# A selective-scan layer with soft-routed experts: a separate buffer for VectorE's product with C, pair-sized dt buffers, the softplus chains placed part by part, y gated in its gate's buffer

## The reference

```
xf, res = split(x @ in_proj.T)                  # 512 channels each
xf = silu(conv(xf));  xb = silu(conv_b(xf))     # causal, 4 taps
per direction (xb: reversed in time):
  delta, B, C = split(u @ x_proj.T)             # 16 states
  dt = softplus(delta @ dt_proj.T + bias)
  dA = dt * A;  dA_cum[l] = exp(sum of dA after l)
  xs = cumsum(dt * u * B * dA_cum) / (dA_cum + 1e-12)
  y  = sum over the states of xs * C,  + u * D
y = (y + y_b) * silu(res);  x1 = layernorm(x + y @ out_proj.T)
x1n = layernorm(x1) * g + b;  logits = x1n @ slots_n.T    # 1024 slots
dispatch = softmax over rows;  combine = softmax over slots
per expert (16, of 64 slots): gelu(s @ Wg + bg) * (s @ Wu + bu) @ Wd + bd
out = layernorm(x1 + combine @ experts)
```

## Time and profile before

| | us |
|---|---|
| median of three runs | 6382.84 (6379.36 to 6392.4) |
| profiled execution | 6391.75 |
| its span | 6389.9 |
| POOL, DVE busy | 4857.2, 4887.0 |
| first scan of the loop, last scan | 99.7, 5290.0 |

### The profile page before, as it was taken

How to read it: one execution, slowest core, us unless ns; L and a number is a source line. 1 busy time by engine, 2 the same in 40 slices (tenths; PEclk the granted TensorE clock), 3 DMA queues, 4 the chain that set the end, 5 groups by cost and what they waited for, 6 DMA issues and landing times. The chain is left out here.

```text
span 6389.9 us, 71120 instructions
## 1 busy us (share of the span) xinstructions
PE 5305.4 (83%) x14640; PEld 2615.8 (41%) x14640; DVE 4887.0 (76%) x4310; ACT 4299.3 (67%) x6698; POOL 4857.2 (76%) x2327
## 2 busy tenths in 40 slices
PE   6878788888878787888888878787878787999977
PEld 2333333333333333334343434343434344555566
DVE  6988888888888888888888888888888882222233
ACT  4878787878778777878787878787878784111100
POOL 3999999999999999999999999999999991000000
PEclk9999998988989888889898989898989898999988
DMA  2434333333333333434343433333333332322266
GB/s 78 123 118 122 120 120 114 120 120 118 120 115 121 115 122 115 122 111 124 114 122 111 124 117 121 115 117 117 121 118 120 121 123 82 95 84 86 75 217 210
DMA packets 555713, 755.58 MB, mean 118 GB/s; under 512 B 124059, under 2 KB 272411, under 8 KB 553245
## 3 DMA queue, kind: packets, MB, share of 16 engines
q1 hardware_dynamic: 555293, 752.04, 38.0%
HBM read 662.04 MB, written 89.82 MB: 118 GB/s over the span
## 5 line engine op out<-in xcount | busy, mean ns | idle before, releaser
L637 POOL TENSOR_TENSOR g_ring<-dtu,b_ring 128x1024 f32<-128x1024 f32 x1026 | 2523.2, 2462 | 148.2 <-DVE e_ps L1008 107.2
L1008 DVE TENSOR_TENSOR_SCAN e_ps<-e_ps,g_ring 128x1024 f32<-128x1024 f32 x1024 | 2342.9, 2288 | 109.0 <-ACT e_ps L802 72.7
L646 POOL TENSOR_TENSOR v_ring<-z_ring,c_ring 128x1024 f32<-128x1024 f32 x896 | 2191.0, 2446 | 144.8 <-PE y_ps L1175 109.4
L1175 PE MATMUL y_ps<-v_ring,ident 128*128 128x512 f32 x3596 | 2036.0, 677 | 305.1 <-POOL v_ring L646 293.4
L802 ACT ACTIVATE e_ps<-dt,a_neg 128x512 f32<-128x512 f32 x2050 | 1398.6, 682 | 808.1 <-DVE z_ring L1025 635.2
L812 ACT ACTIVATE f_ring<-rsum,consts,a_neg_half 128x512 f32<-128x512 f32 x2050 | 1645.6, 803 | 0.8
L1025 DVE SCALAR_TENSOR_TENSOR z_ring<-f_ring,e_ps 128x1024 f32<-128x1024 f32 x896 | 1089.6, 1216 | 388.6 <-PE y_ps L1175 267.9
L1175 PEld LDWEIGHTS y_ps<-v_ring,ident 128*128 128x128 f32 x3596 | 704.8, 213 | 1186.2 <-issue 754.2
L1110 PE MATMUL side<-u,conv_diag 128*128 128x512 f32 x1088 | 503.7, 607 | 31.6 <-ACT rowT_ring L733 31.6
L1285 ACT ACTIVATE x_act<-x_gate,x_bg 128x512 f32<-128x512 f32 x128 | 87.9, 687 | 562.2 <-PE x_gate L1317 562.2
L1140 PE MATMUL side<-seT,xnT 128*128 128x512 f32 x544 | 308.9, 704 | 122.9 <-ACT xnT L727 102.4
(11 more groups left out here) (137 smaller groups left out, 5688.5 us busy)
## 6 DMA issues: line engine op xcount, KB each, us to landing
b_ring<-bc_scr SPq DMA_DIRECT2D x1027, 256.0 KB, 3.4
c_ring<-bc_scr SPq DMA_DIRECT2D x1025, 256.0 KB, 3.3
pT_scr<-rowT_ring SPq DMA_DIRECT2D x136, 256.0 KB, 3.5
m_pT<-pT_scr SPq DMA_DIRECT2D x16, 2048.0 KB, 8.4
sT_scr<-sT_ring SPq DMA_DIRECT2D x272, 64.0 KB, 2.5
x_xT<-sT_scr SPq DMA_DIRECT2D x16, 1024.0 KB, 8.8
eo_scr<-x_eo SPq DMA_DIRECT2D x32, 512.0 KB, 5.1
m_eo<-eo_scr SPq DMA_DIRECT2D x16, 1024.0 KB, 11.0
```

Of the source, the lines that this page charges most:

```text
L637: pool.tensor_tensor(g_ring[:, k], dtu[d][:, pair:pair + 2], both(b_ring[:, k:k + 1]), ALU.mult).then_inc(g_done, 1)
L646: pool.tensor_tensor(v_ring[:, k], z_ring[:, k], both(c_ring[:, k:k + 1]), ALU.mult).then_inc(v_pool, 1)
L1008: dve.tensor_tensor_scan(e, e, g, 0.0, ALU.mult, ALU.add).then_inc(scan_done, 1)
L1175: pe.matmul(y_ps[:, t % 2], ident[:], v, start=(t % (TILES // PAIRS) < 2), stop=True, skip_group_check=True).then_inc(v_used, 1)
```

## The change

Five things are changed, all in `sequence_stage`:

- DVE's product with C goes to a buffer of its own, `v_own`, and PE reads it there. DVE's product waits for PE's use of its previous product. The wait of z for a `z_ring` buffer is now always for POOL.
- `dt`, `dtu` and `rsum` hold one pair of chunks for each direction. Chunk i is at i % 2.
- The table of slots has another order, and `slot_tiles` spreads the slots between given tiles (`EARLIEST`). The dt pairs begin at tiles 1, 34, 66 and 97 (before: 2, 18, 43, 97).
- `yg` is `res_gate`: y is gated in place. res_0 and res_1 leave the slots made ahead (tiles 114, 116); all four res slots come after the out slots, at tiles 13, 16, 20, 23 (res_2 and res_3 before: 12, 15). `X_STEP` is 17.
- The slot embeddings are normalized in `g_ring` instead of `dt[0]`. PE's dt1_0 also waits for the bank of the slot before it.

Some more tiles, before and after: in0_0 31, 37; conv0_0 and conv0_1 37, 39 and 43, 44; rowsT_0 and rowsT_1 41, 42 and 46, 47; colsT_0 47, 48; conv1_0 and conv1_1 52, 54 and 52, 53; x0 88, 89; conv1_2 and conv1_3 91, 93 in both; the last slot 122 in both.

```diff
     order = """
-        dt1_0 dt1_1 out0 out1 res2 res3 dt0_2 dt0_3 xnT0 xnT1
-        rows0 rows1 in0_0 in0_1 cols0 cols1 conv0_0 conv0_1 rowsT0 rowsT1 dt1_2 dt1_3 colsT0 colsT1 rows2 rows3
-        conv1_0 conv1_1 slots0 slots1 cols2 cols3 rowsT2 rowsT3 colsT2 colsT3 rows4 rows5 slots2 slots3 cols4 cols5
-        in0_2 in0_3 rowsT4 rowsT5 conv0_2 conv0_3 colsT4 colsT5 x0_0 rows6 conv1_2 conv1_3 rows7 dt0_0 dt0_1
-        slots4 slots5 x1_0 cols6 cols7 rowsT6 rowsT7 res0 res1 colsT6 colsT7 slots6 slots7"""
+        dt1_0 dt1_1 out0 out1 res0 res1 res2 res3 xnT0 xnT1
+        rows0 rows1 dt0_2 dt0_3 in0_0 in0_1 cols0 cols1 conv0_0 conv0_1 rowsT0 rowsT1 colsT0 colsT1 rows2 rows3
+        conv1_0 conv1_1 slots0 slots1 cols2 cols3 rowsT2 rowsT3 colsT2 colsT3 rows4 rows5 dt1_2 dt1_3 slots2 slots3
+        cols4 cols5 in0_2 in0_3 rowsT4 rowsT5 conv0_2 conv0_3 colsT4 colsT5 x0_0 rows6 conv1_2 conv1_3 rows7 dt0_0 dt0_1
+        slots4 slots5 x1_0 cols6 cols7 rowsT6 rowsT7 colsT6 colsT7 slots6 slots7"""
...
+EARLIEST = {("dt1", 0): 1, ("out", 0): 8, ("xnT", 0): APPLY_TILE + 2, ("dt0", 2): 34, ("dt1", 2): 66, ("in0", 2): 79,
+            ("dt0", 0): 97, ("slots", 7): 122}
+
+
+def slot_tiles(table):
+
+    anchors = [s for s, slot in enumerate(table) if slot in EARLIEST]
+    tiles = []
+    for s, slot in enumerate(table):
+        first = max(a for a in anchors if a <= s)
+        after = min([a for a in anchors if a > s], default=first)
+        tile = EARLIEST[table[first]]
+        if after > first:
+            hold = [HOLD[kind] for kind, _ in table[first:after]]
+            tile += int((EARLIEST[table[after]] - tile) * sum(hold[:s - first]) / sum(hold))
+        tiles.append(max([tile] + tiles[-1:] + [t + 2 for t in tiles[-2:-1]]))
     return tiles
...
-    SP_LAG, X_STEP = 4, 10
+    SP_LAG, X_STEP = 4, 17
...
-        dt = [sb(f"dt{d}", [P, KI, L]) for d in range(NDIR)]
-        dtu = [sb(f"dtu{d}", [P, KI, L]) for d in range(NDIR)]
-        rsum = [sb(f"rsum{d}", [P, KI, L]) for d in range(NDIR)]
+        dt = [sb(f"dt{d}", [P, 2, L]) for d in range(NDIR)]
+        dtu = [sb(f"dtu{d}", [P, 2, L]) for d in range(NDIR)]
+        rsum = [sb(f"rsum{d}", [P, 2, L]) for d in range(NDIR)]
         sp_exp, sp_one = dtu, rsum
-        yg = sb("yg", [P, KI, L])
+        yg = res_gate
...
-                    dve.wait_ge(side_free[at.bank(s)], at.freed(s, 1 - SLOTS // 2))
+                    dve.wait_ge(side_free[at.bank(s)], at.freed(s, 1 if p == 0 else 1 - SLOTS // 2))
...
                 def z_slot_free(i):
 
-                    user = before(i)
-                    if on_dve(user):
-                        dve.wait_ge(v_used, b * TILES + (2 * (user + 1) + CR))
-                    else:
-                        dve.wait_ge(v_pool, b * (STEPS - len(ON_DVE)) + (pool_steps(user + 1) + CR))
+                    dve.wait_ge(v_pool, b * (STEPS - len(ON_DVE)) + (pool_steps(last_on_pool(before(i)) + 1) + CR))
...
-                    z_slot_free(i)
-                    dve.tensor_tensor(z_ring[:, k], e_ps[:, i % 2], both(c_ring[:, k:k + 1]), ALU.mult).then_inc(v_dve, 1)
+                    dve.wait_ge(v_used, b * TILES + (2 * (dve_step_before(i) + 1) + CR))
+                    dve.tensor_tensor(v_own[:], e_ps[:, i % 2], both(c_ring[:, k:k + 1]), ALU.mult).then_inc(v_dve, 1)
...
+                    if (kind, i) == ("dt1", 0):
+                        pe.wait_ge(side_free[at.bank(s - 1)], at.freed(s - 1))
...
-                v = (z_ring if on_dve(i) else v_ring)[:, RING[i % STEPS], t % 2]
+                v = v_own[:, t % 2] if on_dve(i) else v_ring[:, RING[i % STEPS], t % 2]
```

58 lines of the change are left out of this document (22 added, 36 removed).

## The result

The changed kernel takes 6341.46 us (median of five runs, 6329.01 to 6359.75), beside 6391.55 for the kernel before in the same comparison: ratio 0.9927, 95% interval 0.9909 to 0.9944. That is 47 to 50 us won. The forecast was 6297 and a gain of 86 to 95: the direction was right and the time lies in the range, but about half of the expected gain is missing. The question of the experiments is where it went.

The account below looks back on a forecast made before the run. POOL was taken as the bound, busy 303 of about 326 us a sequence, so five waits priced the change: 5.4 us times 16 = 86, from 6391.75 to 6306, then 6297 for the median; range 6165 to 6450.

Parts of the forecast that it names:

- PE 7.7 to 7.2: POOL's idle time from PE's use of v buffers: expected to fall from 7.7 to 7.2 us a sequence.
- the feedback: DVE's own wait on PE had been feeding back into PE's next bank; PE's 7.7 us was left at 7.2.
- the denser turns: PE's turns 43 to 57: 37.1 us of work in the new order, against 35.4 us that POOL needs.
- POOL's load is now the larger in each part: After moving chains, POOL's part loads 83.0, 75.0, 75.0, 70.1 us against DVE's 73.1, 74.9, 72.2, 66.5.
- As the number of such instructions is unchanged, the rule puts nothing into the sum: Two-SBUF-input DVE instructions and GpSimd ones exclude each other; their number is unchanged, so this adds nothing to the forecast.
- The premise that I had set to be tested: Stretching of POOL's instructions is constant: POOL's busy time in the kernel stays within 0.5% of 4857 us.
- The parts: A sequence's four parts of 16 steps: first near 88 us, third near 79, second 78 to 83.
- The reading of the clock: Second part 77.4 or 83.8 us: a few us of half-speed matmuls cost POOL 6.7 us of idle time.
- Rival 3: Slower: PE becomes the bound in turns 43 to 57 and again 83 to 95; 6447 us, chance 0.20.
- Rival 2: The wait only changes hands, POOL waiting for the same late PE one step later; 6383 us, chance 0.12.
- Rival 1: Evening out works fully, DVE never holds POOL, 10 us of 23 idle remain; 6175 us, chance 0.15.
- the stretching: Lengthening of POOL's instructions beside softplus chains; an estimated 1.9 us moves from the first part to the third.

Follow-up runs that it names:

- res_own: res_only with DVE's product with C in a buffer of its own and nothing else; 6253.73 us.
- res_only: The kernel before with all four gate slots together after the out slots and y gated in place, old chains and buffers; 6367.73 us.
- dt1late: res_own with the second pair of dt1 alone moved from tile 43 to 64, part two to part three; 30 us more than res_own.
- res_own_yield: res_own with POOL waiting, before its next product, until DVE's softplus fix step is done; 6228.27 us, ratio 0.9752.
- dt0late: res_own with the second pair of dt0 alone moved from tile 20 to 31, part one to part two; 114 us more than res_own.
- bothlate: res_own with the second pairs of dt0 and dt1 both moved later, old slot function and four-chunk buffers kept; 151 us more than res_own.

## Why the prediction was right or wrong

**What bounds the kernel: right.** In every run POOL is busy for 92 to 96% of a sequence, and its busy time stays within 297 to 303 us. Its idle time after, by the releasers in the groups by line divided by the number of sequences (products g over 64: 9.2, 9.3 and 9.5), beside what was forecast:

```
wait, us a sequence      before   forecast   after   res_own
v on z                    2.2       0          0       1.0
g on the scan             7.3       4.0        9.5     4.9
v on PE                   7.7       7.2        3.4     0.7
B row                     2.5       2.5        2.5     2.0
dtu on rsum               2.7       3.3        4.1     2.6
no releaser shown         0.1       0.1        1.4     1.7
```

**The product's own buffer: right in kind, too small.** z's wait on PE and POOL's wait on z went, as said. But the buffer was worth 114 us on top of the gate's part, not the 86 that all parts were to give. The term that undersized it is "PE 7.7 to 7.2": the feedback, that DVE standing still frees PE's next bank late and PE then holds POOL, is named there, but the denser turns were set against it and half a microsecond was left. From res_only to res_own v's wait on PE falls from 3.3 to 0.7 us a sequence. The larger fall, from 7.7 to 3.3, had come with the gate's slots before that, for which nothing was taken. The scan's wait fell by 2.1 with the buffer alone (7.0 to 4.9), where 3.3 was forecast.

**The softplus chains moved: the step that failed.** I had put the moved chain at POOL's load (two dtu and 1.9 us of stretching, 4.3 us in all), since "POOL's load is now the larger in each part", and had the scan's wait fall. It rose to 9.5 us. The parts one and two together went from 174.9 to 164.6 (-10.3), the parts three and four from 151.0 to 158.1 (+7.1), and dt1late shows the same with one chain alone, -9.2 and +11.8. The long fix isn't all of it: with POOL's wait in both kernels the third part still is 11.0 us longer with the chain than without (78.4 and 67.4). So the moved chain costs its part about DVE's 9.4 us and not POOL's 4.3. The reason fits the rows, but wasn't isolated: the scans that POOL waits for stand behind the chain in DVE's queue, even where DVE isn't full: in the changed kernel's third part it is busy 72.90 of 79.40 us, near the 72.2 forecast. The load of an engine over 16 steps didn't say what a burst of it costs within three.

**"As the number of such instructions is unchanged, the rule puts nothing into the sum": wrong.** Their number is unchanged, their cost is not. It depends on how many products POOL has ready at that moment. The fix took 8.2 us a sequence before and 16.8 after, up to 10.42 at step 20, and taking the shut-out away wins 77 us in the changed kernel and 51 in the one before. So part of the gain seems to be given back by what brought it: once POOL waits less, it runs its products without gaps, and a fix that needs a gap finds none (12.9 to 18.1 us from res_only to res_own). That this is worth the 26 us between 77 and 51 isn't clear of noise. The premise that I had set to be tested, POOL's busy time within 0.5%, moved by -0.6% only. It was the wrong engine to look at; the stretch is in DVE's row L932.

**The parts.** The first, the third and the second were forecast at 88, 79 and 78 to 83; measured on the mean are 81.7, 79.4 and 82.9. The second and third are as said. The first is 6 us better: in the window shown POOL is busy 77.4 us of it, where 83.0 was forecast, since the window holds 46 instructions of POOL instead of 50. For the fourth the prediction gives POOL's load alone, 70.1; the forecast sequence of 320.5 us leaves 70.5 to 75.5 for it, and it took 78.7. Its fix at step 52 takes 4.91 us on average, where it took 1.43. But this isn't all: with the fix at 1.75 in res_own_yield the part still takes 79.0. Part of the difference is POOL's lead at the cut, which this view can't separate.

**The reading of the clock.** The prediction laid all of the 6.7 us between two second parts (77.4 and 83.8) to half-speed matmuls. The fix took 1.21 us in the first of them and 3.38 in the second, so some 2 us can be its own. After, the same two parts are 80.7 and 85.3 long, and the fix took 5.76 and 10.40, which is as large a difference, at the same clocks as before (0.96 and 0.92). What the clock costs POOL by itself isn't shown by these pairs.

**The gate's slots and y in place:** I had taken nothing; res_only has 0.9976 (0.9964 to 0.9988), 15 us faster. POOL's wait on PE fell from 70.4 to 30.4 us in 3000, of which 12.2 came back as idle time before g with no releaser (1.0 to 13.2). xT's later load cost nothing that shows.

**The rivals.** Rival 3, PE as the bound in turns 43 to 57, did not come about: v's wait on PE fell, and half of the conv's matmuls less wins 1.2 to 2.5 us a sequence. In dt0late and bothlate, with a chain beside the conv fills, its mechanism does appear (66.8 and 61.8 us). Rival 2 fell with it. Rival 1, "DVE never holds POOL", is what res_own comes close to without any evening out: 13.6 us of idle time left a sequence, against the 10 that were worked out for it; and 12.5 with the yield. Of the 13.6, 5.9 still are waits on the scan and z.

**The sum.** Idle time fell by 1.3 us a sequence and POOL's busy time by 1.8, the sequence by 3.2, times 16 = 51, beside 47 to 50 measured. That this comes so close is luck: the two profiled executions are only 32 us apart. The forecast was 5.4 of idle time, and nothing of busy time. The time fell inside the stated range because that is wide (6165 to 6450), and not because its terms were right. Two of the prediction's sums are off, too: PE's wait 2 us less gives 6265 and not 6250, and the stretching comes to 1.8 us a chain and not 1.9; neither changes the outcome. In the order of the runs, by ratios: the gate's part -0.24%, the buffer -1.76%, the chains and their new table +1.27%, together -0.73%.

## What to carry to other kernels

A price for a contended instruction is a price for its moment: where VectorE has an instruction with two SBUF operands and GpSimd runs without gaps, look at that instruction's own duration in the trace, and if it is several times the usual one, let GpSimd wait for it by a semaphore just ahead of its next instruction, or take one operand from PSUM. Moving a burst of side work from a full part to an empty one isn't free on an engine that stands in a loop with another: here a burst of 9.4 us made its new part 11 to 15 us longer and its old one 8 to 9 us shorter. And a change in several parts should be run part by part, since here one part won 114 us and the others gave 88 back.

## What was unexpected of the hardware

- An instruction of VectorE of 1.2 us with two SBUF operands was kept out for four GpSimd products in a row, 10.40 us in all (9.2 us of standing), when these followed each other without a gap. In the changed kernel 25 of the 65 fix steps of an execution took over 4 us, before it was one.
- When such an instruction comes first it takes 1.21 us, and GpSimd's product is stretched from 2.35 to 3.24; where it waited for one product and won the boundary (2.59 in all), the next took 3.34. Who wins a boundary between two products changed from sequence to sequence, with nearly the same start inside the product (0.85 and 0.82 us after its begin), and sequences of one execution differed with it by up to 9 us (318.2 and 327.4).
- With one of the two operands in PSUM the same instruction took 1.22 to 1.23 us beside running products, every time.
